# A Fourier mixing stage: row spectra handed over inside the chip's memory, results stored in their place, and the weight ring moved to the other buffer

## The reference, cut to what matters

```python
xn = _layernorm(x, norm1_w, norm1_b)
xf = jnp.fft.rfft2(xn.astype(jnp.float32), axes=(1, 2), norm='ortho')
xf = xf.reshape(B, h, w // 2 + 1, NB, BS)
...
o1 = jnp.einsum('bhwni,hwnio->bhwno', xf, w1c) + b1c
o1 = jax.lax.complex(jax.nn.relu(o1.real), jax.nn.relu(o1.imag))
...
xs = jnp.fft.irfft2(o1, s=(h, w), axes=(1, 2), norm='ortho')
xm = _layernorm(xs, norm2_w, norm2_b)
hdn = jax.nn.gelu(xm @ mlp_w1 + mlp_b1, approximate=False)
return xs + residual + mlp_out
```

## Time and profile before

| | us |
|---|---|
| median of 3 runs (1187.06 to 1192.08) | 1189.72 |
| the profiled execution | 1187.93 |
| its span, first to last instruction | 1186.1 |

### The profile page before, as it was taken

The page is one execution under the profiler, slowest core; times in us unless marked ns, Lnnn a source line. Parts: engine busy times, 40 slices in busy tenths (PEclk is TensorE's granted clock), DMA queues, the critical chain, the costliest instruction groups (busy, mean ns, idle before and its releaser), DMA issues. The chain is left out here.

```text
span 1186.1 us, 25550 instructions
## 1 busy us (share of the span) xinstructions
PE 1068.2 (90%) x9064; PEld 816.2 (69%) x9064; DVE 804.3 (68%) x2102; ACT 725.0 (61%) x1325; POOL 352.8 (30%) x386
## 2 busy tenths in 40 slices
PE   2559999994799999999799999999999599999998
PEld 1249888882487888888555554654654388888887
DVE  4736555641768886776768689699698567666665
ACT  2646565651766667666677576567535266766665
POOL 1260021111322222221238437348157211111110
PEclk9869899996899999999899999999999699999999
DMA  6978699995300000000100000000000000000001
GB/s 138 284 184 159 147 186 182 169 196 155 93 6 0 0 0 0 0 0 0 47 1 1 1 1 1 1 1 1 1 1 0 1 14 27 27 27 27 27 27 40
DMA packets 140280, 64.26 MB, mean 54 GB/s; under 512 B 115856, under 2 KB 134960, under 8 KB 140192
## 3 DMA queue, kind: packets, MB, share of 16 engines
q1 hardware_dynamic: 132888, 37.42, 15.5%
q0 software_dynamic: 5664, 18.83, 6.1%
q10 hardware_dynamic: 1648, 6.91, 1.8%
HBM read 44.27 MB, written 12.58 MB: 48 GB/s over the span
## 5 line engine op out<-in xcount | busy, mean ns | idle before, releaser
L1093 PE MATMUL L_conv_ps<-w2hl,L_conv_hhi 128*128 128x384 f32 x768 | 228.0, 365 | 8.1 <-DVE X L993 7.5
L909 ACT ACTIVATE L_conv_hf<-L_conv_ps,L_conv_b 128x512 f32<-128x512 f32 x192 | 132.1, 688 | 150.9 <-PE L_conv_ps L1074 142.2
L983 DVE TENSOR_TENSOR L_conv_hlo<-L_conv_hf,L_conv_hhi 128x512 fp32r<-128x512 f32 x192 | 140.0, 744 | 103.4 <-ACT L_conv_hhi L918 101.1
L1093 PE MATMUL L_conv_ps<-w2hl,L_conv_hlo 128*128 128x192 f32 x768 | 188.3, 252 | 0.0
L862 POOL TENSOR_TENSOR X<-X,L_conv_b 128x192 f32 x128 | 72.4, 598 | 358.8 <-DVE L_conv_xn L968 358.8
L1208 POOL TENSOR_TENSOR sc_lo<-XS,sc_hi 128x512 fp32r<-128x512 f32 x96 | 141.6, 1490 | 115.6 <-ACT sc_hi L1284 115.6
L1093 PEld LDWEIGHTS L_conv_ps<-w2hl,L_conv_hhi 128*128 128x128 f32 x768 | 144.2, 188 | 14.7 <-DVE L_conv_hlo L983 7.2
L1093 PEld LDWEIGHTS L_conv_ps<-w2hl,L_conv_hlo 128*128 128x128 f32 x768 | 146.1, 191 | 0.0
L639 PE MATMUL psF<-spectrum,X 100*24 100x64 f32 x4352 | 128.4, 290 | 12.3 <-issue 9.0
L1284 ACT ACTIVATE sc_hi<-XS 128x512 fp32r<-128x512 f32 x144 | 87.2, 629 | 82.6 <-DVE XS L1341 29.3
L639 PEld LDWEIGHTS psF<-spectrum,X 100*24 100x24 f32 x4352 | 121.4, 121 | 21.8 <-issue 21.3
(11 more groups left out here) (146 smaller groups left out, 2147.9 us busy)
## 6 DMA issues: line engine op xcount, KB each, us to landing
X<-in_L_conv_w SPq DMA_DIRECT2D x136, 144.0 KB
XS<-in_x POOLq DMA_DIRECT2D x8, 768.0 KB, 7.0
rows_spectrum<-XS POOLq DMA_DIRECT2D x8, 768.0 KB, 4.3
d<-rows_spectrum ACTq DMA_DIRECT2D x8, 768.0 KB, 5.1
X<-in_x SPq DMA_DIRECT2D x8, 768.0 KB, 7.7
out<-X SPq DMA_DIRECT2D x15, 384.0 KB, 2.6
XS<-d POOLq DMA_DIRECT2D x59, 96.0 KB, 4.9
spectrum<-in_L_conv_mlp_w SPq DMA_DIRECT2D x2, 576.0 KB, 9.7
```

The costliest lines, as they stand in the source:

```text
L909: nc.scalar.activation(hf[:, m % 3, :], ps[:, RB + m % 2, :], gelu, bias=b1[:, m:m + 1]).then_inc(act1, 1)
L983: nc.vector.tensor_tensor(hlo[:, m, :], hf[:, m % 3, :], hhi[:, m, :].bitcast(F32), ALU.subtract).then_inc(h_lo, 1)
L1093: mm = pe.matmul(o, x, w, start=(m == 0 and n == 0), stop=(m == MT - 1 and n == 1), skip_group_check=True)
```

## The change

Row spectra no longer go through DRAM. `X` now holds all eight groups' `d2`, and SP copies each `d1` there with eight transfers inside the chip's memory, one for each group: sixteen neighbouring partitions of `d1` to every eighth partition of `d2[g]`. One of the two `d1` slots gets a buffer of its own. Before it issues a step's copies, SP waits for all copies of the step before to have landed, and ACT waits for those of two steps before when it fills a `d1` slot again. A group's result `d3[g]` is written where its `d2[g]` was, so nothing waits for a result buffer. The weight ring moves to `XS`, and so the scatters into `XS` can only start when ring places are free: SP issues all of them after its last weights (60 of 64; ACT issues four), then the MLP's weights. x is loaded again, all eight slabs, in `inverse_rows`.

```diff
-        slab = [XS[:, B * k:B * (k + 1), :] for k in range(XT + 4)]
-        xt, xn, d1 = slab[0:XT], slab[XT:XT + 2], slab[XT + 2:XT + 4]
-        Wt = [X[0:HALF + NH, NT // RING * r:NT // RING * (r + 1), :].rearrange("p a c -> p (a c)").rearrange(
+        d2 = [X[:, B * g:B * (g + 1), :] for g in range(NG)]
+        d3 = [d2[g].rearrange("p b c -> p (b c)") for g in range(NG)]
+        def place(u):
+            return (u + RING - 1) % RING
+        Wt = [XS[0:HALF + NH, NT // RING * r:NT // RING * (r + 1), :].rearrange("p a c -> p (a c)").rearrange(
...
+        slab = [XS[:, B * k:B * (k + 1), :] for k in range(XT + 3)]
+        xt, xn, d1 = slab[0:XT], slab[XT:XT + 2], [slab[XT + 2], sb("d1", [P, B, C])]
...
+        def arrived(eng, n, steps):
+            passed(eng, d2_in[n], 16 * steps * (1 if n < 2 else NG - 2))
...
-            for i in range(STEP):
-                sp.wait_ge(d1_done, 2 * TPB + 2 * i)
-                load_piece(0, i)
-            sp.wait_ge(d2_in[1], 16)
+            for k in range(TPB):
+                sp.wait_ge(d1_done, 4 * (k + 1))
+                for n in range(3):
+                    arrived(sp, n, k)
+                for g in range(NG):
+                    sp.dma_start(d2[g][k:P:TPB].rearrange("p b c -> p (b c)"),
+                                 d1[k % 2][P // NG * g:P // NG * (g + 1)].rearrange("p b c -> p (b c)")
+                                 ).then_inc(d2_in[arrival(g)], 16)
+                for i in {5: (0, 1), 6: (2, 3, 4), 7: (5, 6, 7)}.get(k, ()):
+                    load_piece(0, i)
...
-            for n, (u, half) in enumerate(itertools.product((UNITS - 4, UNITS - 3), range(2))):
-                sp.wait_ge(mixed, STEP * (UNITS - 2) + 2 * n + 1)
-                again(u, half)
...
+            ready(NG - 4)
+            for n, groups in enumerate((NG - 3, NG - 3, NG - 2, NG - 2)):
+                if n > 0:
+                    sp.wait_ge(mixed, STEP * (UNITS - 3 + n))
+                if n == 2:
+                    ready(NG - 3)
+                    for k in range(4):
+                        scatter(sp, NG - 3, k)
+                for g, k in itertools.product(range(groups), (2 * n, 2 * n + 1)):
+                    scatter(sp, g, k)
+            for g, slabs in ((NG - 2, range(TPB)), (NG - 1, range(0, TPB, 2))):
+                ready(g)
+                for k in slabs:
+                    scatter(sp, g, k)
+            for dst, src in sh.mlp_loads("L0_conv_"):
+                sp.dma_start(dst, src).then_inc(sh.raw_in, 16)
...
-                pool.dma_start(F1[:, k, :], d1[k % 2].rearrange("p b c -> p (b c)")).then_inc(f1_out[k % 2], 16)
...
-                        passed(act, f1_out[s], 16 * (k // 2))
+                        for n in range(3):
+                            arrived(act, n, k - 1)
...
-                pe.wait_ge(d2_in[g % 2], 16 * (g // 2 + 1))
+                arrived(pe, arrival(g), TPB)
```

More of the change, by code:

```diff
@@ L148, in __init__ @@
         self.raw = self.spectrum[:, 0:2 * HID + MT * C]
-        self.x_back = [self.sem(f"x_back{r}") for r in range(RING)]
+        self.x_back = self.sem("x_back")
         self.raw_in = self.sem("raw_in")
-        self.rows_in = [self.sem(f"rows_in{k}") for k in range(2)]
-        self.last_in = [self.sem(f"last_in{t_}") for t_ in range(TPB)]
+        self.rows_in = [self.sem(f"rows_in{t_}") for t_ in range(TPB)]
     def load_table(self, n, func):
@@ L337, in load_piece @@
             def load_piece(u, i):
-                r, k, rows = u % RING, i % 2, slice(H // 4 * (i // 2), H // 4 * (i // 2 + 1))
+                r, k, rows = place(u), i % 2, slice(H // 4 * (i // 2), H // 4 * (i // 2 + 1))
                 s, at = (k, WF - 1) if units[u] is None else (units[u][1], 2 * units[u][0] + k)
@@ L354, in _, with ready @@
                     load_piece(u, i)
-            def again(u, half):
-                r = u % RING
-                sp.dma_start(X[:, B * (2 * r + half):B * (2 * r + half + 1), :], x_v[2 * r + half]).then_inc(sh.x_back[r], 16)
-            for n, (u, half) in enumerate(itertools.product((UNITS - 4, UNITS - 3), range(2))):
-                sp.wait_ge(mixed, STEP * (UNITS - 2) + 2 * n + 1)
-                again(u, half)
-            for n, (dst, src) in enumerate(sh.mlp_loads("L0_conv_")):
-                sp.wait_ge(mixed, STEP * (UNITS - 1) + n + 1)
+            def ready(g):
+                sp.wait_ge(d3_v, 2 * (g + 1))
+                sp.wait_ge(d3_a, 2 * (g + 1))
+            ready(NG - 4)
[13 more added lines that the diff above has]
+            for dst, src in sh.mlp_loads("L0_conv_"):
                 sp.dma_start(dst, src).then_inc(sh.raw_in, 16)
[L366 to L369, removed]
         @block.gpsimd
@@ L380, in _ @@
                 load(k)
[L381 to L384, removed]
-                pool.dma_start(F1[:, k, :], d1[k % 2].rearrange("p b c -> p (b c)")).then_inc(f1_out[k % 2], 16)
-            n_vectors = sh.load_vectors(pool)
[L389 to L393, removed]
+            for k in range(XT, TPB):
+                load(k)
+            n_vectors = sh.load_vectors(pool)
             pool.wait_ge(sh.vectors_in, 16 * n_vectors)
@@ L463, in inverse_out @@
                 act.wait_ge(inv_done, 4 * g + j + 1)
-                if g >= 2 and half == 0:
-                    act.wait_ge(sh.rows_in[g % 2], 16 * TPB * (g // 2))
-                nc.scalar.activation(d3[g % 2][:, 384 * j:384 * j + 384], ps[:, 7, 0:384], ACT.Copy).then_inc(d3_a, 1)
+                nc.scalar.activation(d3[g][:, 384 * j:384 * j + 384], ps[:, 7, 0:384], ACT.Copy).then_inc(d3_a, 1)
             spread(0)
@@ L485, in _ @@
             act.wait_ge(d3_a, 2 * NG)
-            for k in (2, 5):
+            for k in range(1, TPB, 2):
                 scatter(act, NG - 1, k)
@@ L570, in inverse_out @@
                 dve.wait_ge(inv_done, 4 * g + j + 1)
-                if g >= 2 and half == 0:
-                    dve.wait_ge(sh.rows_in[g % 2], 16 * TPB * (g // 2))
-                nc.vector.tensor_copy(d3[g % 2][:, 384 * j:384 * j + 384], ps[:, 6, 0:384]).then_inc(d3_v, 1)
+                nc.vector.tensor_copy(d3[g][:, 384 * j:384 * j + 384], ps[:, 6, 0:384]).then_inc(d3_v, 1)
             spread(0)
@@ L626, in products @@
             def products(u):
-                r = u % RING
+                r = place(u)
                 pe.wait_ge(w_in[r], 16 * (STEP + 2) * (u // RING + 1))
@@ L706, in _ @@
             for k in range(TPB):
[L707 to L710 removed]
+                sp.wait_ge(sh.rows_in[k], 16 * NG)
+            for k in range(TPB):
+                sp.dma_start(sh.X[:, B * k:B * (k + 1), :], x_v[k]).then_inc(sh.x_back, 16)
         @block.tensor
         def _(pe):
[L714 to L715 removed]
             for k in range(TPB):
[L717 removed]
+                pe.wait_ge(sh.rows_in[k], 16 * NG)
                 passed(pe, xs_done, 4 * (k - 1))
@@ L869, in _ @@
             if XS is not None:
-                for back in sh.x_back:
-                    pool.wait_ge(back, 2 * 16)
+                pool.wait_ge(sh.x_back, 16 * TPB)
             with pool.Fori(0, N) as i:
```

35 lines of the change are left out of this document (8 added, 27 removed).

## The result

| | before | after |
|---|---|---|
| median, us | 1187.06 (7 runs, 1185.77 to 1192.31) | 1198.13 (7 runs, 1196.77 to 1199.11) |
| span of the profiled execution | 1186.1 | 1197.2 |
| first column product | 76.05 | 91.08 |
| end of unit 14's products | 248.39 | 255.22 |
| first inverse row product | 292.03 | 301.50 |

The ratio is 1.0084, 95% interval 1.0063 to 1.0104: the change makes the kernel 11 us slower. I had said 1192 (1178 to 1206), where the centre counts as no change, with chances of 0.28 for faster, 0.31 for no change and 0.41 for slower. The two spans differ by the same 11.1 us, so the traces can be taken apart. From one row of the table to the next: hand-over **+15.0** (predicted +11.8), columns 164.1 us for 172.3, **-8.2** (-5), seam 46.3 for 43.6, **+2.6** (-4), and all that follows the first inverse row product **+1.6** (0). They sum to 11.1; the prediction's sum was 2.8.

The account below looks back on a forecast made before the run. It took rows to wait on x slabs, columns to be bound by PE, and the seam to leave every engine idle. 1187.9 + 11.8 - 5 - 4 = 1190.7, plus 1.8 for the median: 1192 us, range 1178 to 1206.

Parts of the forecast that it names:

- hand-over: Rows to columns: chained on-chip copies replace DRAM writes and loads, so PE starts columns at 87.8 us, +11.8.
- columns: Column phase: lighter DMA queues return time PE loses to late instructions, at most 7.8 us; taken as -5.
- seam: Unit 14's end to first inverse row product: SP's issues take 38.8 us where 43.6 passed; taken as -4.
- Its waits don't bind: Seam: SP's waits cost nothing unless PE stalls again; with the same 6 us lost, the seam would be 42.8.
- The 6 us of stall in unit 16: Seam: PE's stall, counted as 6 of the 43.6 us before; the middle seam estimate has it gone.
- the predicted 8.1: Row steps of SP's copies: 2.1 + 7 x 0.80 + 0.4 = 8.1 us; bounds 6.3 and 9.3, or 10.0 with x.
- the 0.65 that the prediction itself gave as a sign of being wrong: Hand-over: the prediction is wrong if a copy costs under 0.65 or over 0.95 us.
- The 0.4 us for x: Row steps: the slab of x loading beside the copies adds 0.4 us to the middle estimate, 0.7 to the upper bound.
- ACT's new wait: Rows: ACT's wait for copies two steps back is always over before SP's wait.
- SP's issue bounds the copies: Hand-over rival, chance 0.27: copies overlap, steps take 6.3 us, columns start at 74.4, time 1178 us.
- Sixteen neighbours as the source: Hand-over rival, chance 0.25: sixteen neighbours share too few ways, a step takes 10 us, +25, time 1206 us.
- x loaded again: After the seam: eight slabs need 26 us, POOL wants them 26.4 us after the first inverse row product; cost nothing.

Follow-up runs that it names:

- e3: Changed kernel with POOL issuing the scatters of the odd slabs, except the last group's; 1188.52 us, ratio 1.0007 to the kernel before.
- e1: Changed kernel with two sets of arrival semaphores, so SP waits for the copies of two steps back; 1188.66 us, ratio 1.0000 to the kernel before.
- e9: e6 with the x loads of steps 3 to 7 left out, so its output is not the reference's; 1178.83 us, one run.
- e6: Changed kernel with the edits of both e1 and e2; 1187.64 us, ratio 1.0007 to the kernel before.
- e2: Changed kernel with row-transform columns reordered, so a group's copies leave from every eighth partition; 1195.84 us, ratio 1.0063 to the kernel before.
- e4: Changed kernel with row spectra going through DRAM again, all else as changed; 1188.04 us, ratio 1.0013 to the kernel before.
- e7: e4 plus e3's sharing of the scatters with POOL; 1178.89 us, ratio 0.9941 to the kernel before.
- b1: Kernel before, with POOL scattering groups 0 to 5 only, SP group 6 and group 7's even slabs, ACT its odd slabs; 1180.67 us, ratio 0.9939.
- e5: e6 plus e3's sharing of the scatters with POOL; 1177.52 us, ratio 0.9922 to the kernel before.
- e8: e5 with one DMA a row step in place of eight copies; 1184.39 us, ratio 0.9986 to the kernel before.
- e11: e8 with the one copy a step issued by POOL, behind the loads of x; 1185.03 us, ratio 0.9996 to the kernel before.
- e10: e2 with one DMA a row step in place of eight copies; 1193.83 us, ratio 1.0062 to the kernel before.

## Why the prediction was wrong

- **The step that failed is the seam.** It said "60 x 0.60 = 36.0, then four weight loads, 2.1, drain and release 0.7: 38.8", and took -4. Measured: SP begins 1.2 us after unit 14, the 60 issues take 38.65 (0.644 each, since single ones take up to 1.95), 3.5 more go into two waits for PE's products, where it had "Its waits don't bind", and 2.9 into loads and release: 46.3. A price that a row gave for three issues was multiplied by 60 with no margin and a cover assumed for each wait. e3 shows that the queue is the cause, for with half of it the seam is 36.8. The 6 us of stall in unit 16 did go, as predicted; they were not worth anything, since PE wasn't last. The seam is 6.6 us of the 8.3 by which the sum was short; the misses of the hand-over (+3.2) and of the columns (-3.2) cancel, which is luck.
- **Hand-over, +15.0 for +11.8.** The chain was right and binds (e1), and the step of 8.6 lies beside the predicted 8.1. That is partly luck, for it was put together wrongly: a copy is paced at 0.615 by SP's issue, not at 0.80 by transport, below the 0.65 that the prediction itself gave as a sign of being wrong. Seven copies' pace is then 4.3 us, and the other 4.3 are the landing of the last copy, for which it had 2.1 + 0.4. The 0.4 us for x, which "takes its share of the same engines", is the undersized term: steps beside a load of x take 9.3 to 11.3, and without x loads the step is 5.93 (e9), for 6.98 with them (e6).
- **ACT's new wait, "always over before SP's"**, was not: six refills wait for landings, 30 us in all. In the changed kernel it costs nothing by itself, since it ends with SP's wait for the same copies (39.28 and 39.26 us).
- **The rivals.** That SP's issue bounds the copies was right as a statement on the copies and wrong as a time, for it had 2.1 us of landing behind each burst, and it was 4.3 on the average. Sixteen neighbours as the source cost 2.4 us at the first column product (e2), not the 13 of that rival.
- **Columns, -8.2 for -5.** Right in kind. e4 and e7 bring the loads of row spectra from DRAM back, and with them 5.8 and 7.7 us. The rest, 0.5 to 2.4, would be the scatters that the kernel before has there, but it isn't clear of the difference between those two. PE's stalls of 3.0 us were less than half. With them went the slower clock: in the columns as a whole it was 0.95 and is 0.98.
- **x loaded again, +1.6 for 0.** POOL's first sum starts 27.1 us after the first inverse row product, where it was 26.4, so this cover nearly held. The inverse rows themselves take 0.7 us longer, with the loads beside them. The rest isn't settled.

## What to carry to other kernels

A transfer that stays on the chip isn't cheaper than a trip through DRAM merely because it is shorter: price it by its landing beside whatever else is in flight, and look for who waits for it. A busy DMA engine isn't the limit merely because its share is high: e2 lowered the share between 27 and 50 us from 0.84 to 0.71 and gained 2.4 us. When work is gathered at the end behind one issuing engine, count the issues, multiply by the mean and not by the best, and compare with the time that the compute engines need; sharing them with a second queue was worth 9.6 us here. What an engine drains at a barrier should be issued early: moving POOL's last scatters to SP and ACT in the kernel before gave 6.3 us for a few changed lines.

Three versions beat both kernels and can't be told apart by their intervals: b1 (0.9939), e7 (0.9941) and e5 (0.9922). So the row spectra may stay on chip or not: once SP doesn't wait for every step's landing, what the columns lose by their later start (80.05 for 76.09) they more than get back in their shorter run (163.7 for 171.8) by the profiled executions, of which e7's was its slowest; the medians are 1.4 us apart.

## What was not expected of the hardware

- Copies between partitions beside loads from DRAM move less than writes to DRAM beside them: 4.23 MB for 6.10 in 23 us, both in one queue and at a share of 0.88 and 0.81. The copies take more of the engines' time even alone (266 GB/s at full share, for 327 of loads and writes together), and much more from neighbouring partitions (174). Whether this is in the path, in the engines or in the sixteen partitions written to no run here tells.
- The share of the engines' time isn't always time lost to others: it can exceed 1 (1.05 in e6), and the copies' rate at full share fell from 263 to 215 GB/s when those of two steps could be in flight in place of one (e2, e6).
- The drain of POOL at a barrier took 8.4 to 15.7 us behind scatters (3.4 in the changed kernel, where it issues none) where SP's took 0.12 to 0.37. In b1 it ended at 272.3, though POOL's last issue was at 256.7 and no scatter took more than 11.6 us to land, which makes 268.3 at the latest. What it waits for stays open.
- PE's stall named issue in the last units: 5.96 us before and 5.33 in b1, which load x beside them; 1.1 to 1.5 in e3, e5, e7, e8 and e11, where POOL issues scatters; none in the changed kernel, e1, e2, e4, e6, e9 and e10, where it issues none. That goes with POOL's transfers and the x loads; no run separates the two.
